# A graph sum by one-hot products on Trainium2: which operand stands still, and when the sums are added

## The reference

```python
# layer 0: 3125 nodes of 256, 50000 edges with 64 attributes, src random, dst sorted
messages = concat([norm(x)[src], edge_attr_64], -1) @ W_message
agg = segment_sum(messages, dst)              # then MLP of three layers, two norms
...
# layer 1: the same edges, rows with 32 of 256 entries kept
h_sparse = maxk(norm(x) @ W_neigh, 32)
summed = segment_sum(h_sparse[src], dst); deg = segment_sum(ones, dst)
x = x + norm(x) @ W_self + summed / max(deg, 1)
```

## Time and profile before

| | us |
|---|---|
| median of three runs | 1442.22 |
| profiled execution | 1443.87 |
| its span, first to last instruction | 1442.1 |
| setup | 0 to 36 |
| O0: graph part of layer 0 | 37 to 497 |
| route and experts 0, sparse rows | 498 to 953 |
| O1: graph part of layer 1 | 953 to 1225 |
| route and experts 1 | 1225 to 1442 |

### The profile page before, as it was taken

The page is one execution under the profiler, slowest core; times in us unless marked ns, Lnnn a source line. Parts: engine busy times, 40 slices in busy tenths (PEclk is TensorE's granted clock), DMA queues, the critical chain, the costliest instruction groups (busy, mean ns, idle before and its releaser), DMA issues. The chain is left out here.

```text
span 1442.1 us, 27181 instructions
## 1 busy us (share of the span) xinstructions
PE 1106.3 (77%) x7129; PEld 943.8 (65%) x7130; DVE 727.3 (50%) x2453; ACT 625.4 (43%) x1765; POOL 747.9 (52%) x841
## 2 busy tenths in 40 slices
PE   1288888889998459999994766748988897298870
PEld 1278777779997349999993333327767786187660
DVE  7135666666557642111113799946665244733335
ACT  3656676663223234444443455527653001344330
POOL 6667766666700042222223677447767772167770
PEclk9979999999999559999997799965589895589995
DMA  6645544545510249999994232143333332423237
GB/s 193 167 121 147 139 130 131 135 131 141 144 45 12 77 153 343 356 353 350 349 342 153 64 90 88 55 151 108 113 96 114 117 118 70 158 89 97 95 100 271
DMA packets 186770, 220.02 MB, mean 153 GB/s; under 512 B 69103, under 2 KB 148503, under 8 KB 186382
## 3 DMA queue, kind: packets, MB, share of 16 engines
q1 hardware_dynamic: 148240, 125.81, 27.1%
q0 software_dynamic: 32352, 87.30, 20.5%
q10 hardware_dynamic: 6046, 5.40, 1.2%
HBM read 187.33 MB, written 32.19 MB: 152 GB/s over the span
## 5 line engine op out<-in xcount | busy, mean ns | idle before, releaser
L783 POOL DMA_INDIRECT O0G<-n_rows,src_tab x260 | 250.9, 965 | 121.0 <-issue 83.4
L783 POOL DMA_INDIRECT O1G<-sparse_rows,src_tab x188 | 181.3, 965 | 73.4 <-issue 62.1
L2008 POOL DMA_INDIRECT e0xs<-token_rows,e0idx x60 | 56.7, 945 | 160.7 <-ACT e0idx L2097 157.1
L802 PE MATMUL O0ps_sums<-O0OH,O0G 128*128 128x80 f32 x1040 | 138.8, 292 | 0.1
L2148 DVE TENSOR_TENSOR e0ys<-e0ps_y,NR 128x256 f32<-128x256 f32 x64 | 27.2, 424 | 216.1 <-PE e0ps_y L2067 216.1
L802 PEld LDWEIGHTS O0ps_sums<-O0OH,O0G 128*128 128x128 f32 x1040 | 132.8, 207 | 4.8 <-issue 1.0
L802 PEld LDWEIGHTS O1ps_sums<-O1OH,O1G 128*128 128x128 f32 x752 | 116.9, 242 | 20.9 <-issue 18.3
L802 PE MATMUL O1ps_sums<-O1OH,O1G 128*128 128x80 f32 x752 | 118.1, 326 | 16.0 <-issue 11.6
L2053 PE MATMUL e0ps_h<-e0xT,e0W 128*128 128x128 f32 x1024 | 127.3, 279 | 0.7 <-ACT e0xT L2103 0.6
L2053 PEld LDWEIGHTS e0ps_h<-e0xT,e0W 128*128 128x128 f32 x1024 | 121.7, 195 | 1.5 <-issue 1.4
L2067 PE MATMUL e0ps_y<-e0W,e0hidT 128*128 128x256 f32 x512 | 121.0, 380 | 0.0
(11 more groups left out here) (383 smaller groups left out, 2575.0 us busy)
## 6 DMA issues: line engine op xcount, KB each, us to landing
e0W<-in_L_ffn_w SPq DMA_DIRECT2D x128, 512.0 KB, 5.9
O0EA<-in_edge_attr SPq DMA_DIRECT2D x97, 128.0 KB, 2.6
expert_out<-e0ys SPq DMA_DIRECT2D x64, 128.0 KB
O0G<-n_rows,src_tab POOLq DMA_INDIRECT x260
e1W_all<-in_L_ffn_w SPq DMA_DIRECT2D x16, 256.0 KB, 5.6
n_rows<-NR SPq DMA_DIRECT2D x5, 640.0 KB
token_rows<-O0N SPq DMA_DIRECT2D x25, 128.0 KB, 2.9
m0own<-token_rows SPq DMA_DIRECT2D x25, 128.0 KB, 2.2
```

The lines of the kernel that those rows point to most:

```text
L783: pool.indirect_dma_start(out=self.G[:, s, k, :], out_offset=None, in_=self.rows_dram, in_offset=bass.IndirectOffsetOnAxis(ap=src_tab[:, g ...
L802: last = nc.tensor.matmul(self.ps[o % 2][0:rows.shape[1], half * P:half * P + WINDOW], rows, self.OH[:, h, k, 0:WINDOW], start=(k == 0), s ...
L2008: pool.indirect_dma_start(out=xs[:, s, :], out_offset=None, in_=token_dram, in_offset=bass.IndirectOffsetOnAxis(ap=idx[:, s:s + 1], axis=0 ...
```

## The change

Of a far group, the one-hots become the weights and the gathered rows move.

- **Half groups.** Columns 0 and 1 of a group, and 2 and 3, have bases of their own (`base_half`) and windows of 48 nodes (`HALF_W`). The one-hot has 4 x 48 columns in place of 4 x 80. The first half writes PSUM partitions 0 to 47, the second 64 to 111, so PE's order of columns is 0, 2, 1, 3. Four matmuls move 256 features each, four more (O0 only) the 65 edge columns.
- **Copy and turn.** The sums now have nodes on partitions. ACT copies them to SBUF (`copy`, 112x321 in O0, 112x256 in O1), PE transposes them in three pieces (two in O1) into a bank `ps_turned` (`turn`), and DVE adds two windows of 48, 3x48 elements each, at two bases. In O0 each of these is a slot later than the one before: the add of a far group comes two slots after its products (lag 2). In O1 copy is in the products' slot and turn and add in the next (lag 1). Near groups are added one slot later, as before.
- **Order on DVE in O0.** The load of the first adjacency base, then the one-hot, the loads of the sums' bases, the load of the second adjacency base, the adjacency adds, and the sums adds last.
- **Around it.** Edges are laid into groups column by column (`(c p)` in place of `(p c)`). Setup computes the halves' bases, spans and relative tables. `WINDOW` goes from 80 to 88, which only the limits of the plan use. The gate's logits share a bank with `agg` (O0) or with the turned rows (O1), with a wait each, since `ps_turned` takes a bank. Some small tables move into the space of `w_nodes`, and a triangle of ones (`before`) is built on POOL by the route.

```diff
-WINDOW = 80
+WINDOW = 88
+HALF_W = 48
+HALF_AT = 64
...
 def products(self, pe, o):
...
-                    for half in range(self.halves):
-                        for k in range(GC):
-                            rows = self.EA[:, e, k, :] if half == 2 else self.G[:, r, k, half * P:(half + 1) * P]
-                            last = nc.tensor.matmul(self.ps[o % 2][0:rows.shape[1], half * P:half * P + WINDOW], rows, self.OH[:, h, k, 0:WINDOW],
-                                                    start=(k == 0), stop=(k == GC - 1))
+                    for k in (0, 2, 1, 3):
+                        at = k // 2 * HALF_AT
+                        last = nc.tensor.matmul(bank[at:at + HALF_W, 0:D], self.OH[:, h, k, :], self.G[:, n % self.GR, k, :],
+                                                start=(k % 2 == 0), stop=(k % 2 == 1))
+                    for k in (0, 2, 1, 3) if self.with_edges else ():
+                        at = k // 2 * HALF_AT
+                        last = nc.tensor.matmul(bank[at:at + HALF_W, D:D + DE + 1], self.OH[:, h, k, :], self.EA[:, e, k, :],
+                                                start=(k % 2 == 0), stop=(k % 2 == 1))
...
+            def copy(self, act, o):
...
+                    act.wait_ge(self.summed, o + 1)
+                    if n >= 2:
+                        act.wait_ge(self.turned, n - 1)
+                    nc.scalar.activation(self.R[0:HALF_COLS, n % 2, :], self.ps[o % 2][0:HALF_COLS, 0:self.row_cols], ACT.Copy).then_inc(self.copied, 1)
+            def turn(self, pe, o):
...
+                    pe.wait_ge(self.copied, n + 1)
+                    if n >= 1:
+                        pe.wait_ge(self.added, self.adds_until(self.plan.gathered[n - 1]))
+                    for part in range(self.halves):
+                        cols = min(P, self.row_cols - part * P)
+                        last = nc.tensor.transpose(self.ps_turned[0:cols, part * P:part * P + HALF_COLS], ...)
+                    last.then_inc(self.turned, 1)
...
+            def add_window(self, dve, window, sums):
+                if self.adds_issued:
+                    dve.wait_ge(self.added, self.adds_issued)
+                nc.vector.tensor_tensor(window, window, sums, ALU.add).then_inc(self.added, 1)
...
 def group(q):      # of adds_at, DVE
-                        for o in parts(groups_of(u), q):
-                            sums.hot_and_add(dve, o)
...
                             for v in parts(units_of(u), q):
+                                adjacency.read_base(dve, v, 0)
+                            for o in sums_at(u, q):
+                                sums.hot(dve, o + 2)
+                                sums.read_bases(dve, o)
+                            for v in parts(units_of(u), q):
+                                adjacency.read_base(dve, v, 1)
                                 adjacency.add(dve, v)
+                            for o in sums_at(u, q):
+                                sums.add_all(dve, o)
...
 def group(q):      # of products_at, PE
-                        for o in parts(groups_of(u), q):
-                            sums.products(pe, o)
+                        for o in sums_at(u, q):
+                            sums.turn(pe, o - sums.lag)
+                            if o < sums.groups:
+                                sums.products(pe, o)
```

More of the change, by code:

```diff
@@ L756, in __init__ @@
+                self.R = hot[:, hots:hots + rows].rearrange("p (r d) -> p r d", r=2)
                 self.OH_any = hot[:, 0:GU * GC * P].rearrange("p (h c w) -> p h c w", h=GU, c=GC)
                 self.ps = [pb(f"{tag}ps_sums{b}", [P, 512], c) for b in range(2)]
+                self.ps_turned = pb(tag + "ps_sums_turned", [P, 512], c)
+                self.adds_issued = 0
+                self.lag = 2 if with_edges else 1
+                self.add_order = [i for o in range(self.groups + self.lag) for i in self.adds_at(o)]
@@ L763, in clear, with is_gathered, gathered_before, adds_at @@
             def clear(self, dve):
                 for bank in self.ps:
-                    nc.vector.memset(bank[P // 2:P, 2 * P:3 * P], 0.0)
+                    nc.vector.memset(bank[:], 0.0)
+                nc.vector.memset(self.ps_turned[P // 2:P, 2 * P:3 * P], 0.0)
+            def is_gathered(self, o):
+                return self.plan.sequence[o] >= DENSE_GROUPS
+            def gathered_before(self, o):
+                return sum(self.is_gathered(i) for i in range(o))
+            def adds_at(self, o):
+                far = [o - self.lag] if o >= self.lag and self.is_gathered(o - self.lag) else []
+                near = [o - 1] if 1 <= o <= self.groups and not self.is_gathered(o - 1) else []
+                return far + near
@@ new lines, in read_bases, with add_all @@
+            def read_bases(self, dve, o):
+                for i in self.adds_at(o):
+                    g = self.plan.sequence[i]
+                    if self.is_gathered(i):
+                        self.bases[i] = [dve.value_load(base_half[0:1, g - DENSE_GROUPS, h:h + 1], min_val=0, max_val=NPAD) for h in range(2)]
+                    else:
+                        self.bases[i] = [dve.value_load(base_row[0:1, g:g + 1], min_val=0, max_val=NPAD)]
+            def add_all(self, dve, o):
+                for i in self.adds_at(o):
+                    self.add(dve, i)
@@ L916, in piece, with join @@
                     last.then_inc(self.passed, 1)
[L918 removed]
+            def join(self, dve, q, sums):
                 half_pass = PIECES // 2
@@ L1366, in group @@
                             def group(q):
+                                for o in sums_at(u, q) if adjacency else ():
+                                    sums.copy(act, o - 1)
                                 for v in parts(late_units_of(u), q) if more else ():
@@ L1373, in group @@
                                     adjacency.hot(act, v + HOTS - 1)
+                                for o in sums_at(u, q) if more else ():
+                                    sums.copy(act, o)
                             return group
```

247 lines of the change are left out of this document (155 added, 92 removed).

## The result

The changed kernel took **1482.11 us** (median of four runs, 1477.77 to 1486.12) against 1442.11 of the kernel before: a ratio of 1.0287, 95% interval 1.0269 to 1.0305. (The ratio is that of the timed comparison; the two medians divide to 1.0277.) It is 40.0 us slower; forecast were 24 more (1466, range 1425 to 1500).

What follows compares the result with a forecast made beforehand. DVE's queue, with value loads and waits, was taken to pace O0's unit steps together with PE. From the profiled 1443.9 us, +31 (unit steps), +2 (setup), -4 (steps 17 to 22), -5 (O1), less 1.65, gave 1466 us, range 1425 to 1500.

Steps and rivals of the forecast that it cites:

- Loads: O0 unit steps: one more base load per far group, 0.60 us of DVE's queue, +1.8 us a step.
- Sums adds: O0 unit steps: two adds behind the adjacency adds replace one that cost nearly nothing under loads, +1.9 us a step.
- Waits for PE: O0 unit steps: adds a slot later find products done, so DVE's waits go, -1.9 us a step (-1.0 other end).
- Products: PE, far group: about 2.4 us becomes 1.7 if passes overlap, 2.7 if not; no gain in unit steps.
- Steps 17 to 22: O0 after the unit steps, PE full: shorter products bring -12, cut by POOL's gathers to -4 us.
- Setup: Before O0's steps: extra small operations, table operations, copy, cast and matmuls cost +2 us (1 to 3).
- O1: Stage O1, 47 far groups: POOL's 11.3 us of waits for products go, less a longer tail: -5 us.
- the second paragraph of the prediction: O0: DVE's arithmetic takes 154.8 of 248 us, but with loads and waits for PE it accounts for nearly all.
- the bound of +6: O1: upper end of the range -9 to +6 us, if products come one after the other at clock 0.67.
- Behind O1: After the last copy of O1: no change forecast, 0 us.
- C: Rival for O0: loads are read ahead under arithmetic and POOL's gathers pace; about 1412 us, chance 0.22.
- B: Rival: products don't overlap, PE becomes second pacer; 1480 to 1510, about 1492 us, chance 0.20.

Runs made afterwards that it cites:

- one load, one add: Changed kernel with one value load and one sums add per far group, the second half's sums left out: 1420.42 us, ratio 0.9860.
- two adds, one load: Changed kernel with one value load less per far group, the second half's sums added at the first half's base: 1440.13 us, ratio 0.9983.
- the run with the other order: Changed kernel with PE's columns in the order 0, 1, 2, 3 in place of 0, 2, 1, 3: 1482.86 us, ratio 1.0281.
- few loads: Kernel before with both adjacency bases in one load and no range checks behind DVE's loads in O0 and O1: 1396.15 us; again, 1402.44.

## Why the prediction came out as it did

The forecast was slower, by DVE's queue, with the unit steps of O0 as the place. That holds. The 40 us can be walked through in runs that each add one part of the change (medians of different sets of runs, so that each step is good to a few us):

| from | to | median, us | step | 21st copy of O0, us |
|---|---|---|---|---|
| | before | 1442.1 | | 421.7 |
| before | new order on DVE | 1428.4 | -13.7 | -16.3 |
| new order | products turned, one load, one add | 1420.4 | -8.0 | -4.4 |
| one load, one add | two adds | 1440.1 | +19.7 | +14.4 |
| two adds, one load | two loads: the change | 1482.1 | +42.0 | +40.5 |

(The step from one add to two is that between the two runs with one load. Added first, without the second load, it costs 19.7; taken away from the whole change it brings 33.6, the load 28.1 behind it in place of 42. The two together are certain, the split depends on which comes first.)

*Loads: the mechanism right, the term too small.* +1.8 us a step was counted for the 17 unit steps (50 groups, 31 us); it measured 40.5 in O0. The place was right: 36.5 of it lie before the 16th copy and 4.0 in the steps behind, where nothing was counted. What fell short is the size in the unit steps, 0.76 us a group where 0.60 was taken; POOL's waits for products went from 74.0 to 34.0 with that load, and PE's for the adjacency adds from 59.0 to 38.1. With one add in place of two a load is worth less, 0.51 us a group there and 0.17 behind (counted from the first gather in both runs). Why it is more than its length in the one case and less in the other isn't shown.

*Sums adds: right in sign, wrong in its reason.* +1.9 a step was put on the place behind the adjacency adds. The place is a gain: -13.7 us in the kernel before. What costs is the second add, +19.7. The step of the prediction that failed is the sentence that the old add "cost nearly nothing" because it ran under loads. It did run under them, but with its wait for the products (11.3 in the earlier trace rows) it stood ahead of the adjacency adds, on which PE's counts hang. That this price is part of the 31.0 and 25.8 of the earlier trace rows is an inference from the run with the new order, in which all three waits shrink.

*Waits for PE: -1.9 a step.* DVE's 17.8 and 13.6 are gone but for 0.7. What that is worth was not measured apart: the new order alone took 16.3 off O0, and DVE's waits for PE fell by the same 16.3 there (31.4 to 15.1), while 32 was counted. (The term's division is off, too: at 17.6 us a step, 95 to 335 us hold 13.6 steps and not 15, which makes -2.1 a step.) In the forecast the sums adds (+32) and the waits (-32) cancel. In the runs the second add (+14.4 in O0, taken ahead of the second load) and the new order (-16.3) nearly cancel as well, each at about half of its forecast size. That the sum was left to the loads was luck in this.

*Products: 1.7 us a group, right.* From the turns' start to the next work it is 1.64 us (267.39 to 269.03). It was put down to passes that run side by side, and they do, two at a time, in 0.90 us where 1.1 was estimated. That the columns must alternate between the halves for it isn't so: the run with the other order has pairs too. Of the two sentences of the Trainium skill that were weighed ("TensorEngine Tiling (Array Packing)", section "Tiling Modes"), the first, that different tiles may multiply in parallel, agrees with these pairs, though the trace doesn't name the tiles. Of the second, a drain at the change of mode, little can be seen: the three turns and the change behind them take 0.41 us, and three turns at 0.11 would be 0.33.

*Steps 17 to 22: -4, measured -3.9*, but as a sum of two: with one load and one add the turned form brings -8.5 there (78.4 to 69.9), and loads and adds take half of it back.

*Setup: +2*, measured 2.3: the first gather starts at 41.55 in place of 39.27. One pair of profiles doesn't fix this closely: in other runs with the changed setup it starts at 40.8 to 44.6, with the old one at 39.3 to 43.0.

*O1: -5, measured +3.8, wrong.* The 11.3 us of POOL's waits for products were expected to go and rose to 17.6. Load and add hold DVE there too: with one of each O1 takes 232.9, and 246.8 with two. The term counted what PE wins and left DVE's +0.9 a group (0.60 + 0.26) uncounted because DVE was busy only 86 of 135 us, which is the very error that the second paragraph of the prediction warns of for O0. That the bound of +6 held it was luck: it was put there for slow products.

*Behind O1: 0, measured +2.3*: some 1.7 from the last copy to the route (copy, turn and adds of the last groups, counted in O1's tail) and 0.8 in the route. The triangle of ones is now built on POOL there (0.6 us); that this is the cause was not shown.

*The rivals.* C (loads read ahead) asked for more than half of the added time to be hidden; the unit steps grew instead, and a load there cost 0.5 to 0.8 us a group. The measured time lies in B's range (1480 to 1510, PE as second pacer) as well as in the forecast's own (1450 to 1485), so the time alone doesn't decide between them. The mechanism does: PE needs 1.64 us a group, not 2.7. POOL's waits for products did not shrink, as forecast: they rose from 31.7 to 74.0.

What stays open: how much of the 46 us that the kernel before wins with few loads belongs to the pairs and how much to the range checks was not measured apart; by the traces, a load with its check holds the queue 0.62 us, without it 0.36, a load of two values without checks 0.57.

## What to carry to other kernels

An engine with half of its time idle can be the bound: add what its queue does between instructions (value loads, range checks, waits of one add for the other) before calling it free. Where the queue is what everybody waits for, price each at about its full length, even if the trace shows arithmetic over some of them: here a load of 0.62 us cost 0.5 to 0.8 a group there, and 0.2 where the queue had room. In a ring of engines that wait for each other, put first the result that the next round hangs on, here the counts, and last the one that has a bank to spare. Before shortening the busiest engine's work, ask what a step takes when it waits for nobody: here a change of the loads alone brought 3%, and both forms of the products came out alike.

## What the runs showed of the hardware

A range check nearly doubles the price of a value load: the load itself takes 0.30 us, the register work and the assertion behind it 0.19 and 0.02, and with the gaps it is 0.62 from one load to the next, against 0.36 without the check. A load of two values takes 0.53; with what follows it holds the queue 0.57 without checks and 1.12 with them. Passes of 256 fp32 columns through 48 columns of weights ran two at a time, started 0.007 us apart where the program alternated between the halves and 0.014 where it did not, and at the full clock pairs followed each other as closely (0.215 us) as single passes through 128 columns do.
